# Attention prologue of a two-layer fused kernel: x in halves, first four heads first, second batch's split on ScalarE and GpSimd

## What is computed

```python
mod = (_silu(L0_c) @ L0_wmod).reshape(2, 6, 1, -1)
sa, ca, ga, sb, cb, gb = (mod[:, i] for i in range(6))
h = _layernorm(x) * (1 + ca) + sa
q = (h @ Wq.T).reshape(N, S, 16, 8).transpose(0, 2, 1, 3)   # k and v alike
energy = jnp.einsum('nhqd,nhkd->nhqk', q, k)
attn = jax.nn.softmax(energy / jnp.sqrt(8.0), axis=3)
out = jnp.einsum('nhql,nhld->nhqd', attn, v)
```

## Time and profile before

| what | value |
|---|---|
| median of 3 runs | 1132.33 us (1130.43 to 1132.64) |
| the profiled execution, its own time | 1135.81 us |
| its span in the profile | 1134.5 us |
| mean granted TensorE clock | 0.941 |
| busy: PE, DVE, ACT, POOL | 92%, 85%, 72%, 46% |
| tensor reductions of the first pass | 256, mean 1214 ns |
| exponentials of the second pass | 512, mean 599 ns |
| first product of the first pass | at 30.73 us |
| first score of the second pass | at 60.94 us |

### The profile page before, as it was taken

One profiled execution on the slowest core, in us unless ns is written; L12 is line 12 of the kernel. 1 busy time (PEld: TensorE's weight loads), 2 busy tenths in 40 slices (PEclk: granted clock), 3 DMA queues, 4 the chain that ended last, 5 costly groups with the idle time before them and its releaser, 6 DMA issues. The chain is left out here.

```text
span 1134.5 us, 21410 instructions
## 1 busy us (share of the span) xinstructions
PE 1043.9 (92%) x7835; PEld 650.8 (57%) x7835; DVE 969.5 (85%) x1327; ACT 818.4 (72%) x1593; POOL 517.9 (46%) x487
## 2 busy tenths in 40 slices
PE   6899999999999887989999999899999996599997
PEld 4222222222222333458988984468888984388896
DVE  6899999999995676979999996989999999866666
ACT  3279898999999544978888854888888833246652
POOL 5400441010101111027889982048999974146663
PEclk9779999999999888799999999899999997699999
DMA  5210100001004420107999980118999977512224
GB/s 158 71 44 15 30 16 17 29 16 31 16 2 76 131 57 2 59 1 191 241 249 226 221 210 3 59 28 191 232 246 230 229 184 259 131 50 64 62 64 126
DMA packets 60313, 121.04 MB, mean 107 GB/s; under 512 B 15471, under 2 KB 28783, under 8 KB 59953
## 3 DMA queue, kind: packets, MB, share of 16 engines
q0 software_dynamic: 15440, 52.66, 23.2%
q1 hardware_dynamic: 43064, 64.82, 18.6%
q10 hardware_dynamic: 1704, 2.20, 0.6%
HBM read 58.02 MB, written 13.19 MB: 63 GB/s over the span
## 5 line engine op out<-in xcount | busy, mean ns | idle before, releaser
L2267 PEld LDWEIGHTS m_pair<-filter_w,delta_x_t 128*128 128x128 f32 x2560 | 294.0, 192 | 43.3 <-issue 43.3
L2267 PE MATMUL m_pair<-filter_w,delta_x_t 128*128 128x112 f32 (+3 forms) x2560 | 298.7, 276 | 9.4 <-DVE h_t L2294 4.1
L570 DVE TENSOR_REDUCE neg_max<-max_ps 128x1 f32<-128x1024 f32 x256 | 293.5, 1214 | 10.8 <-PE max_ps L559 10.5
L686 ACT ACTIVATE exp_scores<-score_k 128x512 f32<-128x512 f32 x512 | 273.9, 599 | 20.7 <-PE score_k L678 13.4
L2243 ACT ACTIVATE decay<-delta,a_log 128x1024 f32<-128x1024 f32 x128 | 145.7, 1142 | 50.0 <-DVE normed L2294 28.7
L559 PE MATMUL max_ps<-k_rows,q_rows 48*128 48x512 bf16 x512 | 166.8, 404 | 7.7 <-DVE neg_max L570 6.5
L2235 ACT ACTIVATE filter_w<-filter,b_t 128x112 f32<-128x112 f32 (+1 forms) x576 | 167.4, 374 | 0.0
L706 PE MATMUL score_k<-exp_scores,v_cols 128*32 128x256 f32 x2048 | 165.1, 396 | 0.0
L678 PE MATMUL score_k<-q_rows,k_rows 51*128 51x512 bf16 x512 | 162.8, 391 | 0.6 <-DMA q_rows<-neg_max_rows 0.6
L579 POOL CAST neg_max_parts<-neg_max 128x16 bf16<-128x16 f32 x16 | 3.1, 196 | 228.8 <-DVE neg_max L570 228.8
L559 PEld LDWEIGHTS max_ps<-k_rows,q_rows 48*128 48x128 bf16 x512 | 30.1, 95 | 120.6 <-DVE neg_max L570 91.9
(11 more groups left out here) (343 smaller groups left out, 1726.9 us busy)
## 6 DMA issues: line engine op xcount, KB each, us to landing
c_row<-c_rows SPq DMA_DIRECT2D x64, 512.0 KB, 6.3
x_inner<-normed POOLq DMA_DIRECT2D x16, 512.0 KB, 6.7
delta_x<-mod_memory POOLq DMA_DIRECT2D x15, 512.0 KB, 8.0
delta_x<-x_inner POOLq DMA_DIRECT2D x15, 512.0 KB, 9.0
x_inner<-h_t POOLq DMA_DIRECT2D x14, 512.0 KB, 6.5
mod_memory<-h_t POOLq DMA_DIRECT2D x14, 512.0 KB, 9.1
mod_memory<-normed POOLq DMA_DIRECT2D x12, 512.0 KB, 9.3
gate_up_all<-in_gate_up_w SPq DMA_DIRECT2D x8, 512.0 KB, 7.5
```

Of the source, the lines that this page charges most:

```text
L570: ve.tensor_reduce(nm[leg % 2][:, 4 * j + qt:4 * j + qt + 1], mps[:, bank:bank + 2, :].rearrange("p a q -> p (a q)"), AX_X, ALU.max, negat ...
L686: ac.activation(pt[a % 4][:, HEADS[r % 4], :], eps[:, bank, :], ACT.Exp, scale=SC).then_inc(*exped.up())
L2267: mm = pe.matmul(vps[blk][:, lo:hi], self.duT[b][:, c, blk * P:(blk + 1) * P], wf[g % 3][:, lo:hi], start=True, stop=True)
```

## The change

1. x of the first batch is loaded in two halves of 256 KB, normed by halves (`in_x_first`, `in_x_next`). The second batch's x is issued after seven small loads. The second layer's modulation matrix is loaded after the bf16 identity has been made. VectorE reads the modulation columns after the eight normed tiles, not before.
2. In the first batch (`first_batch_parts`) VectorE makes the rests, one middle part and the last low part; ScalarE makes the other three middle parts; GpSimd three low parts.
3. Only four heads' parts are written and loaded first. The low parts of heads 0 and 2 go from SBUF to SBUF by four DMAs (L906), without DRAM. The other twelve heads' parts are written after the loads of the first group.
4. `silu_c` of layer 1, its spread, all constant fills of GpSimd come before the second batch. The second batch's projections, values, `mod_row(1)` and `pe_mod_cols(1)` are emitted between tiles 0 to 12 of the first pass, a piece behind each tile. Its rest is a copy of the PSUM bank by ScalarE and a subtraction by GpSimd (`ac_part_copy`, `po_part_rest`), its middle part ScalarE's, its low part GpSimd's.
5. The maxima of leg 0 are turned behind tile 17, not 18, and their four DMAs are issued by SyncE and ScalarE, two each.

```diff
-        for b in range(NB):
-            sp.dma_start(self.X[:, b * TB:(b + 1) * TB, :],
...
+        for half in range(2):
+            lo = half * TB // 2
+            sp.dma_start(self.X[:, lo:lo + TB // 2, :], A["L0_attn_x"][0][lo * P:(lo + TB // 2) * P].rearrange(
+                "(k p) d -> p k d", p=P)).then_inc(*self.in_x[half].up(16))
...
+            def put_max_turn(leg):
+                for engine, heads in ((sp, (1, 0)), (ac, (3, 2))) if leg == 0 else ((sp, range(4)),):
...
-            self.ac_silu_c(1)
...
+            self.ac_load_modulation(1)
+            half = TB // 2
+            roots = [self.ln_root(self.X, i * half, (i + 1) * half, [self.in_x[i].at()]) for i in range(2)]
+            self.po_spread(0)
+            normed = [self.ve_ln_apply(self.X, t, roots[t // half]) for t in range(TB)]
+            self.ve_mod_cols(0, cols_ps)
+            scaled = self.m_scale
+            root = self.ln_root(self.X, TB, NT, [self.in_x[2].at()])
...
+                def first_batch_parts():
+                    tiles, rest_in = [(c, side) for c in range(2) for side in range(2)], []
+                    for n, tile in enumerate(tiles):
+                        bank = ring.take()
+                        pe_project(*tile, bank)
+                        ac_part_hi(*tile, bank)
+                        rest_in.append(ve_part_rest(*tile, bank))
+                        if n == 0:
+                            po_part_lo(*tile, ve_part_mid(*tile, rest_in[0]))
+                        if n > 1:
+                            po_part_lo(*tiles[n - 1], ac_part_mid(*tiles[n - 1], rest_in[n - 1]))
+                    ve_part_lo(*tiles[3], ac_part_mid(*tiles[3], rest_in[3]))
...
+                def second_batch_mid():
+                    tile, rest_in = rest_known.pop()
+                    po_part_lo(*tile, ac_part_mid(*tile, rest_in))
+
+                def second_batch_parts(c, side):
+                    bank = ring.take()
+                    pe_project(c, side, bank)
+                    ac_part_hi(c, side, bank)
+                    ac_part_copy(c, side, bank)
+                    rest_in = po_part_rest(c, side, bank)
+                    if rest_known:
+                        second_batch_mid()
+                    rest_known.append(((c, side), rest_in))
...
+                sp_parts_out(0, range(4), ((part_hi.at(),), (part_mid.at(), part_ve.at())))
...
+                        engine.dma_start(rows[8 * i:8 * i + 8, s], p[2][16 * s:16 * s + 8, side, 0:S]).then_inc(
+                            *first_half.up(16))
...
+                self.ac_silu_c(1)
+                rows_in[0] = [self.mod_row(0, j) for j in range(4)]
+                self.po_spread(1)
                 po_value_columns()
+                po_ones(2, NS)
...
+                for v in range(AHEAD):
+                    ahead(v)
+                    if v < 4:
+                        second_batch_parts(2 + v // 2, v % 2)
+                    elif v < 6:
+                        if rest_known:
+                            second_batch_mid()
+                        values(v - 2)
+                    elif v < 10:
+                        rows_in[1].append(self.mod_row(1, v - 6))
+                    elif v == 10:
+                        cols_ps = self.pe_mod_cols(1)
+                    elif v == 12:
+                        self.ve_mod_cols(1, cols_ps)
```

More of the change, by code:

```diff
@@ L648, in max_turn @@
                 ac_max_turn(leg, bank)
-                sp_max_turn(leg)
+                put_max_turn(leg)
                 idle_banks.append((bank, turn_read.at()))
@@ L861, in attention @@
+                self.po_spread(1)
                 po_value_columns()
+                po_ones(2, NS)
                 ve.wait_ge(*self.ln_aggr.at())
                 normed += [self.ve_ln_apply(self.X, t, root) for t in range(TB, NT)]
-                self.turn(normed, col(1), col(0), (scaled,), done=ht, by=(0, 0, 0, 1), chunks=(2, 3))
-                rows_in[1] = [self.mod_row(1, j) for j in range(4)]
-                self.ve_mod_cols(1, self.pe_mod_cols(1))
-                ahead(0)
-                project(2)
@@ L869, in attention @@
-                ahead(1)
-                ahead(2)
-                project(3)
-                for c in range(2, NC):
-                    values(c)
-                sp_parts_out(1)
-                po.wait_ge(*part_lo.at())
-                po_ones(2, NS)
-                sp.wait_ge(*rows_set.at())
+                self.turn(normed, col(1), col(0), (scaled,), done=ht, by=(0, 0, 0, 0), chunks=(2, 3))
+                for v in range(AHEAD):
[12 more added lines that the diff above has]
+                        self.ve_mod_cols(1, cols_ps)
@@ L881, in attention @@
+                sp_parts_out(1, range(H), ((part_hi.at(),), (part_mid.at(),), (part_po.at(),)))
             gated = self.sig("attn_gated")
-            pe.wait_ge(*self.identb_set.at())
-            for v in range(3, AHEAD):
-                ahead(v)
             for m in v_ready:
```

133 lines of the change are left out of this document (71 added, 62 removed).

## The result

The changed kernel takes **1150.37 us** in the median of 6 executions (1148.54 to 1152.14), against 1132.34 us (1130.43 to 1135.05, 6 executions) for the kernel before on the same chip: ratio 1.0159, interval 1.0141 to 1.0177. It is slower by 18.0 us, where 3.8 us less was forecast. The profiled execution took 1150.28 us, with a span of 1149.0 us and a mean granted clock of 0.933.

What follows compares the result with a forecast made beforehand. All three engines are full in the second pass, so only its start counts; GpSimd's fills set the pace at tile 9. First score moves from 60.94 to 57.1, 3.8 us less: 1132.33 becomes 1128.5, range 1122.5 to 1133.0.

Steps and rivals of the forecast that it cites:

- The way to the first high part: Prologue: halved x gains 0.9 us, later second loads 0.7, moving the first high part from 14.58 to 13.0.
- that VectorE reads the columns after the normed tiles costs nothing: Prologue: free if the normed tiles are done by 9.2 us; 0.3 us if GpSimd's second root holds them up.
- The first batch's parts: Prologue: ScalarE becomes the chain; the last low part ends near 19.0 us, a gain of 1.4 to 1.8 us.
- T: Start of the first high part; last low part ends nearer T+6.2 by the shared-port rule, T+5.9 by a cast's time.
- The DMAs up to the first pass: SyncE's queue: all issued by 23.8 us, first product near 25.7 instead of 30.73, bounds 24.5 and 27.
- 11 x 0.32: SyncE's queue: eleven DMAs, the four direct ones included, priced at a row load's issue time, within a sum of 4.7 us.
- a wait for the bank behind tile 8: First pass: late GpSimd keeps TensorE from a bank until 40.0 us, so reduction 9 comes at 41.5, not 36.9.
- between 35 and 38: First pass: when, in us, TensorE would reach the modulation row behind tile 8, by the clock in the first tiles.
- B: Rival, chance 0.20: TensorE's clock halves while it waits, adding 3 us between tiles 8 and 11; gain 0 to 2.
- D: Rival, chance 0.15: clock falls at 24 us and stays half under the interleaved work; slower, 1140 us.
- D's own sum: Half-clock first pass: tiles 0 to 5 at 2.7 us each, tile 11 near 55.8, first score at 68.5, 7.5 later.
- Should come out at the end of the kernel one for one: Second pass: time saved at its first score, 60.94 us before, appears in full at the kernel's end; 3.8 us.

Runs made afterwards that it cites:

- r_after: The changed kernel itself, run again on the chip of the follow-up runs: 1133.58 us, ratio 1.0124 to the kernel before.
- e1: The changed kernel with six unread products filling TensorE's two pauses around the second batch's transposes: 1119.55 us, ratio 1.0014 to the kernel before.
- e9: e3 with two unread products in the pause ahead of the second batch's transposes: 1116.29 us, ratio 0.9989 to the kernel before.
- r_block: The same program as e3, run once more with 12 executions: 1116.07 us, ratio 0.9986 to the kernel before.
- e2: The changed kernel with second-layer modulation rows and columns back ahead of tile 0, other pieces still between tiles: 1118.6 us, ratio 1.0013 to the kernel before.
- e8: The changed kernel's own instructions and pauses, with the pieces in one block behind tile 0: 1128.41 us, ratio 1.0098 to the kernel before.
- e4: The changed kernel with the second batch in blocks as before, rests still by ScalarE's copy and GpSimd's subtraction: 1117.67 us, ratio 1.0004 to the kernel before.
- e5: The changed kernel, pauses kept, with three unread products once behind tile 0's pair: 1122.98 us, ratio 1.0036 to the kernel before.
- e6: e2 with two unread products in the pause ahead of the second batch's transposes: 1117.3 us, ratio 1.0015 to the kernel before.
- e3: The changed kernel with the second batch in blocks and its rests by VectorE, both as before: 1116.54 us, ratio 0.9993 to the kernel before.
- e7: e3 with an unread product of 256 columns ahead of each pair of tiles 3 to 21: 1120.53 us, ratio 1.0015 to the kernel before.

## Why the prediction was wrong

**The way to the first high part**: 13.60, not 13.0, of 14.58. The transposes start at 8.60, as worked out (0.9 us for the first half of x, and the matrix half a microsecond sooner: silu at 5.76 and the columns' products at 6.02). The step that failed is "that VectorE reads the columns after the normed tiles costs nothing": GpSimd's second root held the last four normed tiles up by 0.65 us, so the columns were read at 10.13 and h_t started at 10.59, which leaves 1.0 us of the 1.6.

**The first batch's parts.** The last low part starts 5.35 us behind the first high part and ends at 19.95, 0.95 later than forecast, of which 0.6 is the later start. VectorE's row, and GpSimd's beside it:

```profile
18.95 1.00 DVE L826 TENSOR_TENSOR part<-part_rest,part 128x512 bf16<-128x512 f32 x1 [0.69 <-ACT part L814]
...
17.13 2.28 POOL L820 TENSOR_TENSOR part<-part_rest,part 128x512 bf16<-128x512 f32 x2 [0.51 <-ACT part L814]
```

GpSimd's third low part ends at 19.41, 0.46 us into VectorE's. The 1.00 us is 0.46 and 0.54, as if VectorE had begun when GpSimd ended. That fits the rule of the Trainium skill (SBUF — State Buffer, SBUF: two separate sides) that the forecast weighed, and its end at T + 6.2 is nearer to the measured T + 6.35 than the T + 5.9 from the rows. The eleven other traces of the new front (r_after, e1 to e9, r_block) have the same pair, and in all twelve the duration less the overlap is 0.54 or 0.55 us, also in e2, where the overlap is 0.34 and the duration 0.88. No trace has this subtraction without GpSimd beside it, so how long it takes alone isn't shown.

**The DMAs up to the first pass.** Forecast: SyncE done at 23.8, first product at 25.7. SyncE's queue:

```profile
21.37 1.17 SPq L524 DMA_DIRECT2D k_rows<-qk_parts  x3
22.64 1.40 SPq L906 DMA_DIRECT2D k_rows<-part  x2
24.14 1.29 SPq L906 DMA_DIRECT2D q_rows<-part  x2
25.48 0.80 SPq L524 DMA_DIRECT2D k_rows<-qk_parts  x2
26.33 0.64 SPq L524 DMA_DIRECT2D q_rows<-qk_parts  x2
```

Done at 26.97. The step that failed is "11 x 0.32": the four direct DMAs take 1.40 / 2 = 0.70 and 1.29 / 2 = 0.65 each, near the 0.60 of a write and not the 0.32 of a load, which is 1.4 us; the loads take 0.39, 0.40 and 0.32 (0.4 us in all), small gaps between them add 0.3, and the queue began late (21.37, where 20.2 was forecast). The last load's issue starts at 26.67 and it is there 1.9 us later, as forecast (1.8); but the forecast had counted the 1.8 from the end of that issue, 0.3 too late. Together the first product is 2.9 us late, outside the stated bound of 27. Against 30.73 it is still 2.2 us earlier: this gain is real, and nearly all that the front gives.

**GpSimd.** It began with the second batch at 32.90, not 31.3, inside the bounds: silu came at 22.51 instead of 21.5, the ones ended at 32.34. The mechanism that was to follow, a wait for the bank behind tile 8, didn't occur: at half clock TensorE came there at 52.42, long after the bank was free (both reads of the values ended by 47.3). The forecast wrote that TensorE would be there "between 35 and 38"; even e1, at full clock and with a first product at 28.37, is there at 41.26, since a step is 1.59 us and not the 1.3 to 1.5 taken. The wait is real only in e8. There it also shows that the forecast had the bank wrong by one: TensorE goes on at 41.70, while ScalarE still reads the second bank of values until 42.24 (40.80 + 1.44), so the row behind tile 8 takes the first of the two banks, which is free some 0.7 us sooner, and the row behind tile 9 the last.

**The clock**, which decided. The step that failed is the pace of TensorE between the tiles: the forecast's sum has it behind tile 8 between 35 and 38 and takes the row there at 0.85 and a pair at 0.6, the prices of full clock. It came there at 52.42, after seven steps of 2.97 us at a granted clock of 0.50. The forecast was B and D's mechanism in 0.35 of its chances, and gave the case that came, D, 0.15. Its argument against D was that "at 28 us the clock was back after 4 us of continuous work". That row is right, and it is about solid work: modulation rows behind modulation rows. The order of instructions, shown ahead of the prediction, says that the change puts a pair between all such pieces, and e2 against e4, e5 and e8 show that this is what makes the difference. The second slip lies ahead of it: the text names the pause before the second transposes, and not that the moved rows and columns had filled the next one (5.4 us of work). With them moved, TensorE waits out the whole way of the DMAs, 4.2 us. What this cost: e1 has 15.3 us in the first exponential and r_after against it 14.0 us in the median.

**D's own sum** came to a first score at 68.5, and it ran at 73.59, 5.1 us later: 2.9 from the first product, 1.6 from six steps of 2.97 where 2.7 was taken (a projection takes 2.07, not 1.7), 0.8 between tile 6 and tile 11 (steps of 2.96 and 2.12 where 2.7 and 1.9 were taken), and 0.3 less behind it. To the 12.6 us at the first score came 1.4 us in the second pass, 0.4 behind it, and the 3.5 us by which the profiled execution lay over its median. In the same way the forecast's first score, 57.1, is missed by 16.5: reduction 9 ran at 55.49, not at 41.5 (3.3 of this from the first reduction, the rest from nine steps), and 2.5 us more went with the columns at half clock (2.72, and VectorE idle 2.39) and reductions of 1.23.

The Trainium skill (TensorE: Matmul & The Clock Gate, Part 1: The HAM clock gate) has the clock depend on recent activity. The falls behind pauses agree with it. Why the clock fell at 30.3 to 31 us in the middle of work in five traces, and why 28.00 busy microseconds of 28.00 (32 to 60 us) left the clock at half, where two projections in a row brought it back (e4), no run here shows.

**"Should come out at the end of the kernel one for one"** failed too. A later start did come out (12.6 at the start, 14.1 at the end), but an earlier one is not sure to: 2.4 us in e1 gave 0.3, and 4.3 us in e6 gave 1.1, while 3.4 us in e3 gave 4.0. These are single executions, and the clock between 120 and 200 us moves each by some microseconds. So even without the fall the forecast's 3.8 us might have come out as less.

**Against the list of signs**, the one that held was D's: granted clock 0.5 from 26 us on, though for about 57 us and not until 45. The range, 1122.5 to 1133.0, left the case out on purpose, with too small a chance.

## What to carry to other kernels

When work is moved out of a place where TensorE would otherwise wait, ask what TensorE's clock does in the hole that is left, and look at the form of the work that follows: a block of products brought the clock back in every run, while small pieces between bf16 pairs kept it at half for as long as they lasted, with records that say busy all the time. Fill a long pause of TensorE that stands ahead of the work that counts (e1), and not its short waits in a stretch where VectorE is the bound (e7). And before counting an earlier start of a full stage as a gain, look at which clock it starts with.

## What the runs showed of the hardware

- One order of the same instructions ran at 0.50 for 28.9 us (28.58 to 57.50, r_after likewise) and at 1.00 in 15.6 us (e1, 28.37 to 44.01); which of the two was settled by what TensorE did ahead of it.
- The same program took 1115.0 to 1117.6 us in six executions and 1122.8 to 1128.3 in four (e6). Traces of such orders differ in whether the clock falls at 30.3 to 31 us, in continuous work (it does in e2, e4, e7, e9 and r_block, not in e3 and e6; e3 and r_block are one program). That all of the longer executions do so is inferred from their times.
- In the second pass, rounds of score pairs and value products at half clock brought the clock back 3.7 us behind the first value products in the changed kernel (79.25 to about 82.9), and 7.7 us behind them in e6 (62.63 to about 70.3).
- VectorE's subtraction with both inputs in SBUF took 0.54 or 0.55 us more than its overlap with a GpSimd subtraction in all twelve traces that have it (1.00 us with an overlap of 0.46, 0.88 with 0.34).
- A DMA of 8 partitions from SBUF to SBUF took SyncE 0.65 to 0.70 us to issue, a row load from DRAM 0.32 to 0.40.
